# The two halves of each scan group: summed by two TensorE matmuls instead of one GpSimd addition, with step orders and dataless matmuls set anew

## The chip, the cores and the metric

The kernel runs on one core of one Trainium2 chip. The metric is the device time of one execution in microseconds (us), median over the runs. It is set against the same kernel before the change.

## The reference, cut to what matters

The program runs 16 batch elements through four blocks: (a) a selective state-space layer, (b) a routed feed-forward layer, (c) a gated delta rule with an inversion of triangular matrices, and (d) attention with a mixture of eight experts. The change is in block (a). There each of 256 inner channels has 16 states:

```
def step(h, inp):
    dt_t, B_t, C_t, u_t = inp
    dA = jnp.exp(dt_t[:, :, None] * A)
    h = h * dA + (dt_t * u_t)[:, :, None] * B_t[:, None, :]
    y = jnp.einsum('bcs,bs->bc', h, C_t)
    return (h, y)
_, ys = jax.lax.scan(step, h0, xs)
y = jnp.swapaxes(ys, 0, 1) + u * D_skip
```

The sum over the 16 states `s` in the line of `y` is what the change moves from one engine to another.

## The kernel before, in words

**The scan.** Channels lie on the 128 partitions in two blocks (`CB = 2`), time (256) along the free axis. The 16 states are taken in eight groups of two (`SG = 2`, `NG = 8`). A group is a tile of 128 x 1024 float32: two states by two channel blocks by 256 time steps. For group st:

- TensorE spreads the row of B over all partitions (`spread` into bank 0), and the row of C (into bank 1).
- ScalarE makes `decay` (L664, four instructions). VectorE makes `drive` (L1378) from bank 0, runs the recurrence into `state[st % 2]` (L1390), and in `a_read` multiplies that state by C in place (L1398).
- GpSimd adds the two halves of the read-out state into `ypart` (L558), and TensorE adds `ypart` into bank 2 with an identity as weights (L887, one matmul 128x512 float32; the trace has two records for each float32 matmul).

There are two `state` buffers. So the recurrence of group st may only overwrite its buffer once the sum of group st-2 has read it. After the last group `a_y` (L1404) takes bank 2.

**The order of work.** There is no scheduler at run time. Each engine runs its own fixed list of steps: the loop over elements runs the first half (blocks a, b and the projections of c; letter x) of element i among the second half (the rest of c, and d; letter y) of element i-1. A string of x and y for each engine (`TURNS`) says whose next step comes. Within a half the steps keep their order. Every engine works in order and waits at semaphores (`wait_ge`). The first half of element 0 runs alone ahead of the loop, the second half of the last element alone behind it.

Beside the scans in the loop stands the inversion of block c: for each of five levels and two chunks, TensorE's `lev_Z`, VectorE's masking `lev_Z` (L1564), TensorE's `lev_TT` (both L1020 on TensorE) and VectorE's transposition `lev_T` (L1560); then `c_R`, `c_top`, `c_low`, `c_X`, `c_U`, `c_O`, `c_S`, `c_kS`, which apply it.

**Dataless matmuls.** `keep_warm` (L1040) issues matmuls whose result nobody reads, ahead of some of TensorE's steps; the table `WARM` says how many at which step, 50 in an element.

Of the kernel before, what the change touches and what calls it, by code (L numbers as in the profile page):

```python
# [114 lines left out]
for e in range(E1):  # L115
    EXPERTS += [("d_down", e, 0), ("d_down", e, 1)]
    if e + 2 < E1:
# [11 lines left out]
        "yyyyyxyxyyyyyyxxyyyyyxyyyyxyxyyyxyxyyyyxxyyyxxyyxxyyxxyxyxxyxxxxyxyxxyyxxxxyxxxyyxyyyxyyxyyxxyyy"  # L129
        "yyxyxyyyyxyyxyyxyyxyyxyyyxxyyyxxxyyyyyyyxx"),  # L130
    "vector": (
        "xyxyyyxyyxyyxyyyyxxyyyxyyxyyxyyxyyxyyxyyxyyxyyxxyxyxxxyxyxxxxxxyxyxxyxyxxyxyxyxxyxxxyxyyxxxyyyxy"
        "xxxyxxxxyxyxxxyxyxxyyyy"),
    "scalar": (
        "yyxxyyxxxxxyyyxyyyyyxxyyxyyxyxxxyxxyxxxyxxyyyxyxyyxxyxyxyyxyyxxyyxyxyxxxyyxyxyxyyxxx"),
    "gpsimd": (
        "yyxxyyyyyyxxxxxxxxxxyyxyxxx"),
# [4 lines left out]
    ("a_xproj",): 2, ("a_out",): 2, ("b_turn",): 1, ("b_logits",): 1, ("c_prod", 2, 0): 1, ("c_prod", 2, 1): 1,  # L142
    ("lev_Z", 0, 0): 2, ("lev_TT", 0, 0): 2, ("lev_Z", 1, 0): 1, ("lev_TT", 1, 0): 2, ("lev_TT", 1, 1): 1,
    ("lev_Z", 2, 1): 2, ("lev_TT", 2, 0): 1, ("lev_TT", 2, 1): 2, ("lev_Z", 3, 1): 2, ("lev_TT", 3, 0): 2,
    ("lev_TT", 3, 1): 1, ("lev_Z", 4, 1): 1, ("lev_TT", 4, 0): 3, ("lev_TT", 4, 1): 1, ("c_X", 0): 3, ("c_O", 0): 1,
    ("c_S",): 1, ("c_kS",): 1, ("c_top", 1): 1, ("c_low", 1): 1, ("c_O", 1): 2, ("c_turn_o",): 2, ("c_out",): 1,
    ("d_scores",): 2, ("d_turn_p",): 1, ("d_av",): 1, ("d_a",): 2,
# [1599 lines left out]
```

## Time and profile before

| what | value |
|---|---|
| device time, median of 3 runs | 2814.28 us (2812.36 to 2824.87) |
| the profiled execution's own time | 2817.26 us |
| its span | 2815.5 us |
| TensorE matmuls busy | 2434.8 us, 86% of the span |
| VectorE busy | 2208.3 us, 78% |
| ScalarE busy | 1197.7 us, 43% |
| GpSimd busy | 605.6 us, 22% |
| mean granted TensorE clock | 0.931 of full speed |
| DMA, mean | 8 GB/s |

Two engines are busy most of the span, and neither all of it. A busy share is a mean over stages with different limits, so what an edit is worth has to be read from the stage in which it lies. The profiled execution stands 3.0 us above the median.

### The profile page before, as it was taken

How to read it: one execution, taken by the hardware profiler on the slowest of the kernel's cores; microseconds unless marked ns; L12 is line 12 of the kernel's file. 1: busy time of each engine (PE TensorE's matmuls, PEld its weight loads, DVE VectorE, ACT ScalarE, POOL GpSimd, SP SyncE). 2: the span in 40 equal slices, each digit the busy share in tenths (PEclk: the TensorE clock that was granted, in tenths of full speed). 3: DMA queues.
4: the chain of work that ended last, by engine and by line, in shares of the span. 5: the costliest groups of instructions: out<-in, count | busy, mean ns of one | idle time of the engine just before them, and what ended most of it. 6: DMA issues, size and time to landing. Idle time of an engine off the chain costs nothing.

```text
span 2815.5 us, 60867 instructions
## 1 busy us (share of the span) xinstructions
PE 2434.8 (86%) x22584; PEld 1890.6 (67%) x22584; DVE 2208.3 (78%) x5056; ACT 1197.7 (43%) x2697; POOL 605.6 (22%) x465
## 2 busy tenths in 40 slices
PE   4688989888898888989888898988889888898987
PEld 2466767667686766768667686766768666676875
DVE  6677887878879787887978779787887978788742
ACT  3233536435263542536444253543526354353612
POOL 2122221221322122231222222122131212223100
PEclk7689999989999999999999999999999999999987
DMA  4000000000000000000000000000000000000000
GB/s 132 4 2 3 7 4 1 8 3 7 3 7 2 3 8 3 7 4 1 8 3 8 3 7 4 1 8 3 7 3 7 2 3 8 3 7 2 1 6 2
DMA packets 24831, 21.41 MB, mean 8 GB/s; under 512 B 7217, under 2 KB 21570, under 8 KB 24530
## 3 DMA queue, kind: packets, MB, share of 16 engines
q1 hardware_dynamic: 24530, 17.26, 2.2%
q8 instruction: 205, 3.36, 0.5%
q14 instruction: 96, 0.79, 0.1%
HBM read 15.13 MB, written 2.13 MB: 6 GB/s over the span
## 4 chain that ended last, share of the span: by engine, by line
issue 42%; PE 25%; DVE 23%; POOL 6%; ACT 1%; DVEq 0%; POOLq 0%; ACTq 0%
PE banks L1048 4%; PE banks L887 3%; PE banks L1020 3%; DVE wide L1390 3%; PE banks L1012 2%; DVE wide L1398 2%; DVE inv L1560 2%; POOL lg L562 2%; DVE inv L1564 2%; DVE wide L1378 2%; POOL rq L534 2%; PE banks L1001 1%; PE banks L1040 1%; DVE inv L1551 1%; PE banks L864 1%
## 5 line engine op out<-in xcount | busy, mean ns | idle before, releaser
L558 POOL TENSOR_TENSOR wide<-wide 128x512 f32<-128x512 f32 x128 | 215.3, 1682 | 782.0 <-DVE wide L1398 428.4
L1513 DVE SCALAR_TENSOR_TENSOR wide<-pad,conv,wide 128x256 f32<-128x256 f32 x864 | 369.5, 492 | 0.0
L1390 DVE TENSOR_TENSOR_SCAN wide<-wide 128x1024 f32<-128x1024 f32 x128 | 294.3, 2300 | 1.9 <-ACT wide L664 0.3
L1040 PE MATMUL banks<-hideb,identb 128*128 128x512 bf16 x800 | 276.1, 402 | 0.0
L1184 PE MATMUL banks<-inv,up 128*128 128x256 f32 x1024 | 265.9, 391 | 0.0
L1194 PE MATMUL banks<-down,inv 128*128 128x128 f32 x2048 | 257.2, 277 | 0.0
L1194 PEld LDWEIGHTS banks<-down,inv 128*128 128x128 f32 x2048 | 250.7, 192 | 5.9
L1020 PEld LDWEIGHTS banks<-inv 64*64 64x64 f32 x5120 | 164.4, 136 | 111.4 <-issue 111.4
L792 ACT ACTIVATE inv<-banks,up1b 128x256 f32<-128x256 f32 x512 | 206.7, 481 | 65.0 <-PE banks L1184 63.3
L1020 PE MATMUL banks<-inv 64*64 64x64 f32 x5120 | 182.2, 222 | 57.8 <-DVE inv L1564 57.8
L664 ACT ACTIVATE wide<-small,a_neg 128x255 f32<-128x255 f32 x512 | 214.4, 496 | 35.7 <-DVE wide L1390 35.5
L1184 PEld LDWEIGHTS banks<-inv,up 128*128 128x128 f32 x1024 | 184.6, 193 | 21.0 <-issue 0.2
L745 ACT COPY inv<-banks 128x512 f32<-128x512 f32 x160 | 91.3, 580 | 242.0 <-DVE inv L1560 209.5
L1020 PEld LDWEIGHTS banks<-inv,mats 64*64 64x64 f32 x5120 | 163.8, 136 | 35.4 <-issue 35.4
L1020 PE MATMUL banks<-inv,mats 64*64 64x64 f32 x5120 | 180.6, 221 | 4.6 <-DVE inv L1557 4.6
L1378 DVE TENSOR_TENSOR wide<-banks,small 128x1024 f32<-128x1024 f32 x128 | 154.2, 1205 | 3.4 <-PE banks L864 3.4
L534 POOL TENSOR_TENSOR vscale<-vscale,expo 128x16 f32<-128x16 f32 x16 | 46.3, 2895 | 506.8 <-DVE rq L1522 506.8
L1398 DVE TENSOR_TENSOR wide<-banks,wide 128x1024 f32<-128x1024 f32 x128 | 154.2, 1204 | 1.0
L1689 DVE SCALAR_TENSOR_TENSOR inv<-banks,gt,inv 128x128 f32<-128x128 f32 x256 | 77.1, 342 | 98.9 <-PE banks L1194 98.9
L864 PE MATMUL banks<-bc,sel3b 96*128 96x256 bf16 x512 | 100.5, 285 | 55.9 <-DVE wide L1378 31.4
L968 PEld LDWEIGHTS banks<-ones_col,wide 128*128 128x128 f32 x1024 | 135.0, 200 | 9.4 <-issue 2.2
L887 PE MATMUL banks<-wide,con 128*128 128x512 f32 x256 | 138.6, 634 | 0.3 <-POOL wide L558 0.3
(277 smaller groups left out, 4846.7 us busy)
## 6 DMA issues: line engine op xcount, KB each, us to landing
gates_bc<-gate_rows SPq DMA_DIRECT2D x32, 128.0 KB, 2.9
x<-in_x SPq DMA_DIRECT2D x16, 128.0 KB, 2.1
up<-in_W SPq DMA_DIRECT2D x1, 2048.0 KB
out<-xn_y SPq DMA_DIRECT2D x16, 128.0 KB, 2.0
wide<-in_wmod SPq DMA_DIRECT2D x2, 384.0 KB, 5.3
con<-in_con SPq DMA_DIRECT2D x1, 724.0 KB, 4.5
w_k<-in_Wk SPq DMA_DIRECT2D x1, 512.0 KB
w_q<-in_Wq SPq DMA_DIRECT2D x1, 512.0 KB
```

The source lines that it names most:

```text
L558: g.tensor_tensor(ypart[p % 2], r[:, 0:512], r[:, 512:1024], ALU.add).then_inc(a_yp.h, 1)
L664: last = s.activation(decay[st % 2][:, at + 1:at + T], dt[:, c, 1:T], ACT.Exp, scale=a_neg[:, c, st * SG + q:st * SG + q + 1])
L792: s.activation(hm[e % 2][:, m, :], bank(3 + half, T, q * T), ACT.Relu, bias=up1b[:, HB1 * e + m:HB1 * e + m + 1]).then_inc(d_hid.h, 1)
L887: t.matmul(bank(2), ident, ypart[st % 2], start=st == 2, stop=st == NG + 1).then_inc(a_yq.h, 1)
L1020: last = t.matmul(PS[a:b, out, h * HALF:(h + 1) * HALF], weights(h, a, b), values(h, a, b), start=True, stop=True)
L1040: t.matmul(bank(bk), identb[:], hideb[:].unsqueeze(1).broadcast_to([P, HG, P]), start=True, stop=True)
L1184: last = t.matmul(bank(3 + half, T, q * T), up1[:, e, m * P:(m + 1) * P], xxT, start=True, stop=True)
L1194: last = t.matmul(bank(bk, D, j * D), hm[e % 2][:, m, j * P:(j + 1) * P], down1[:, HB1 * e + m, :], start=m == 0, stop=m == HB1 - 1)
L1378: v.tensor_tensor(drive[st % 2].rearrange("p (q c t) -> p q c t", q=SG, c=CB), bank(0).rearrange("p (q t) -> p q t", t=T).unsqueeze(2).bro ...
L1390: v.tensor_tensor_scan(state[st % 2], decay[st % 2], drive[st % 2], 0.0, ALU.mult, ALU.add).then_inc(a_h.h, 1)
L1398: v.tensor_tensor(r, bank(1).rearrange("p (q t) -> p q t", t=T).unsqueeze(2).broadcast_to([P, SG, CB, T]), r, ALU.mult).then_inc(a_rd.h, 1)
L1513: v.scalar_tensor_tensor(dst, src, w, dst, ALU.mult, ALU.add).then_inc(c_conv.h, 1)
```

## The change

In step st of TensorE's `a_read`, one matmul on GpSimd's sum becomes two matmuls, one on each half of the state tile that VectorE has read out, both added into bank 2. GpSimd's step `a_scan` goes, with its buffer `ypart` and its semaphore. VectorE's recurrence of group st now waits for TensorE's semaphore `a_y_summed_ps` of group st-2, where it waited for GpSimd's `a_y_pair`. Three pairs of semaphores are merged into shared ones with counts (`c_solve_ps`, `d_qkv_ps`), with the same waits. The turns of all four engines are written anew, and so is the table of dataless matmuls (51 in an element instead of 50).

```diff
@@ gpsimd
-            def a_scan(i, st):
-                if 1 <= st <= NG:
-
-                    p = st - 1
-                    g.wait_ge(a_rd.h, a_rd.at(i, p + 1))
-                    if p >= 2:
-                        g.wait_ge(a_yq.h, a_yq.at(i, p - 1))
-                    r = state[p % 2]
-                    g.tensor_tensor(ypart[p % 2], r[:, 0:512], r[:, 512:1024], ALU.add).then_inc(a_yp.h, 1)
-
@@ tensor, a_read
                 if st + 1 < NG:
                     t.wait_ge(a_rd.h, a_rd.at(i, st + 1))
                     spread(NS + (st + 1) * SG, 1).then_inc(a_C.h, 1)
-                if st >= 2:
-
-                    t.wait_ge(a_yp.h, a_yp.at(i, st - 1))
-                    t.matmul(bank(2), ident, ypart[st % 2], start=st == 2, stop=st == NG + 1).then_inc(a_yq.h, 1)
+                if 1 <= st <= NG:
+
+                    t.wait_ge(a_rd.h, a_rd.at(i, st))
+                    for n in range(2):
+                        last = t.matmul(bank(2), ident, state[(st - 1) % 2][:, 512 * n:512 * n + 512], start=st == 1 and n == 0,
+                                        stop=st == NG and n == 1)
+                    last.then_inc(a_yq.h, 1)
@@ vector, a_scan
                     if st >= 2:
-                        v.wait_ge(a_yp.h, a_yp.at(i, st - 1))
+                        v.wait_ge(a_yq.h, a_yq.at(i, st - 1))
                     v.tensor_tensor_scan(state[st % 2], decay[st % 2], drive[st % 2], 0.0, ALU.mult, ALU.add).then_inc(a_h.h, 1)
@@ TURNS (gpsimd's shown; tensor, vector and scalar are rewritten too)
     "gpsimd": (
-        "yyxxyyyyyyxxxxxxxxxxyyxyxxx"),
+        "yyxyyyyyyxyyxyxxx"),
```

**What the new orders do on VectorE.** In the loop, around the recurrences of groups 5, 6 and 7 (L1390 before, L1382 after; drive is L1378 and L1370, read-out L1398 and L1390, the solve's small steps the rest), VectorE's list was:

```order
L1390 SCALAR_TENSOR_TENSOR wide<-wide 128x1024 [waits a_y_pair,a_drive,a_decay]
L1375 REGISTER_ALU
L1378 TENSOR_TENSOR wide<-banks,small 128x1024 [waits a_state,a_B_spread]
L1398 TENSOR_TENSOR wide<-banks,wide 128x1024 [waits a_C_spread,a_state]
L1390 SCALAR_TENSOR_TENSOR wide<-wide 128x1024 [waits a_y_pair,a_drive,a_decay]
L1375 REGISTER_ALU
L1378 TENSOR_TENSOR wide<-banks,small 128x1024 [waits a_state,a_B_spread]
L1608 TENSOR_TENSOR inv<-banks,rq 128x256 [waits c_O_ps]
L1398 TENSOR_TENSOR wide<-banks,wide 128x1024 [waits a_C_spread,a_state]
L1582 TENSOR_TENSOR inv<-banks,eGS 128x256 [waits c_kS_ps]
```

and is now:

```order
L1382 SCALAR_TENSOR_TENSOR wide<-wide 128x1024 [waits a_y_summed_ps,a_drive,a_decay]
L1367 REGISTER_ALU
L1370 TENSOR_TENSOR wide<-banks,small 128x1024 [waits a_state,a_B_spread]
L1390 TENSOR_TENSOR wide<-banks,wide 128x1024 [waits a_C_spread,a_state]
L1382 SCALAR_TENSOR_TENSOR wide<-wide 128x1024 [waits a_y_summed_ps,a_drive,a_decay]
L1367 REGISTER_ALU
L1370 TENSOR_TENSOR wide<-banks,small 128x1024 [waits a_state,a_B_spread]
L1390 TENSOR_TENSOR wide<-banks,wide 128x1024 [waits a_C_spread,a_state]
L1600 TENSOR_TENSOR inv<-banks,rq 128x256 [waits c_O_ps]
L1574 TENSOR_TENSOR inv<-banks,eGS 128x256 [waits c_kS_ps]
```

The recurrence's wait names another semaphore, and the small step L1600 (`c_o`, L1608 before) has moved from ahead of the read-out to behind it. Between the read-out of group 5 and the recurrence of group 6 nothing stands, before and after.

Around group 3's recurrence, one masking step of the inversion's last level (L1564 before, L1556 after) stood ahead of it and one behind it. VectorE's list now has, from group 2's recurrence to group 3's:

```order
L1382 SCALAR_TENSOR_TENSOR wide<-wide 128x1024 [waits a_y_summed_ps,a_drive,a_decay]
L1370 TENSOR_TENSOR wide<-banks,small 128x1024 [waits a_state,a_B_spread]
L1390 TENSOR_TENSOR wide<-banks,wide 128x1024 [waits a_C_spread,a_state]
L1555 REGISTER_ALU
L1556 TENSOR_TENSOR inv<-banks,con 128x512 [waits c_Z_ps]
L1555 REGISTER_ALU
L1556 TENSOR_TENSOR inv<-banks,con 128x512 [waits c_Z_ps]
L1382 SCALAR_TENSOR_TENSOR wide<-wide 128x1024 [waits a_y_summed_ps,a_drive,a_decay]
```

Both maskings now lie between a read-out and the next recurrence, and none between a recurrence and its read-out. For all six recurrences that wait, the steps between the read-out ahead and the recurrence are now: group 2: two `lev_T`; 3: two `lev_Z`; 4: `c_R`; 5: `c_U`; 6: none; 7: `c_o` and `c_R`.

**What they do on TensorE.** Behind the last product of `c_S` (L1048 before, L1040 after) stands the step that follows group 5's read-out; `spread` is L864 before and L853 after. Before:

```order
L1048 MATMUL banks<-inv,ktok 128x32
L864 MATMUL banks<-bc,sel3b 128x256 [waits a_read]
L864 MATMUL banks<-bc,sel3b 128x256
L887 MATMUL banks<-wide,con 128x512 [waits a_y_pair]
L877 REGISTER_ALU
L864 MATMUL banks<-bc,sel3b 128x256 [waits a_drive]
```

and now:

```order
L1040 MATMUL banks<-inv,ktok 128x32
L853 MATMUL banks<-bc,sel3b 128x256 [waits a_read]
L853 MATMUL banks<-bc,sel3b 128x256
L877 MATMUL banks<-wide,con 128x512 [waits a_read]
L877 MATMUL banks<-wide,con 128x512
L866 REGISTER_ALU
L853 MATMUL banks<-bc,sel3b 128x256 [waits a_drive]
```

The sum is two matmuls in place of one. In front of it stands, as before, the spread of the next C row, which waits for VectorE's read-out of group 5 itself, while the sum is that of group 4.

## Rows read from the trace of the kernel before

**Rows 1.** The page: span, busy engines, and chain that ended last.

```profile
span 2815.5 us, 60867 instructions
...
PE 2434.8 (86%) x22584; PEld 1890.6 (67%) x22584; DVE 2208.3 (78%) x5056; ACT 1197.7 (43%) x2697; POOL 605.6 (22%) x465
...
issue 42%; PE 25%; DVE 23%; POOL 6%; ACT 1%; DVEq 0%; POOLq 0%; ACTq 0%
```

**Rows 2.** Groups by line: busy us, mean ns of one, idle before.

```profile
L1390 DVE TENSOR_TENSOR_SCAN wide<-wide 128x1024 f32<-128x1024 f32 x128 | 294.3, 2300 | 1.9 <-ACT wide L664 0.3
...
L558 POOL TENSOR_TENSOR wide<-wide 128x512 f32<-128x512 f32 x128 | 215.3, 1682 | 782.0 <-DVE wide L1398 428.4 <-PE banks L887 353.6
...
L887 PE MATMUL banks<-wide,con 128*128 128x512 f32 x256 | 138.6, 634 | 0.3 <-POOL wide L558 0.3
```

**Rows 3.** Stretches of one element: length, then busy us of each engine.

```profile
1056.00:1080.00 24.00, 23.82 (x247) 18.01 (x245) 23.47 (x23) 7.35 (x18) 10.03 (x6) 1.00 0.00 1
...
sum 170.00, PE 149.46 PEld 116.84 DVE 140.31 ACT 77.31 POOL 37.80; mean PE 16.61 PEld 12.98 DVE 15.59 ACT 8.59 POOL 4.20
```

**Rows 4.** Timeline after one read-out: start us, length us, engine, line.

```profile
1063.72 1.23 DVE L1398 TENSOR_TENSOR wide<-banks,wide 128x1024 f32<-128x1024 f32 x1
...
1064.96 0.42 DVE L1600 TENSOR_TENSOR inv<-banks,cU 128x256 f32<-128x256 f32 x1
1065.00 0.11 PEld L864 LDWEIGHTS banks<-bc,sel3b 96*128 96x128 bf16 x2 [0.19 <-DVE wide L1398]
1065.01 0.39 PE L864 MATMUL banks<-bc,sel3b 96*128 96x256 bf16 x2
...
1065.23 1.03 PE L887 MATMUL banks<-wide,con 128*128 128x512 f32 x2
...
1065.77 2.28 DVE L1390 TENSOR_TENSOR_SCAN wide<-wide 128x1024 f32<-128x1024 f32 x1
1066.10 0.38 PE L864 MATMUL banks<-bc,sel3b 96*128 96x256 bf16 x2
```

**Rows 5.** Timeline of VectorE and TensorE among inversion steps.

```profile
1037.75 1.15 PE L1020 MATMUL banks<-inv 64*64 64x64 f32 x32 [0.78 <-DVE inv L1564]
...
1043.87 0.67 DVE L1564 TENSOR_TENSOR inv<-banks,con 128x512 f32<-128x512 f32 x1
1044.47 0.70 DVE L1560 STREAM_TRANSPOSE inv<-banks 128x512 f32<-128x512 f32 x1
...
1045.10 1.18 DVE L1398 TENSOR_TENSOR wide<-banks,wide 128x1024 f32<-128x1024 f32 x1
```

**Rows 6.** Timeline of VectorE ahead of the last scan.

```profile
1073.53 0.41 DVE L1608 TENSOR_TENSOR inv<-banks,rq 128x256 f32<-128x256 f32 x1
1073.86 1.21 DVE L1398 TENSOR_TENSOR wide<-banks,wide 128x1024 f32<-128x1024 f32 x1
1074.99 0.41 DVE L1582 TENSOR_TENSOR inv<-banks,eGS 128x256 f32<-128x256 f32 x1
...
1076.11 2.28 DVE L1390 TENSOR_TENSOR_SCAN wide<-wide 128x1024 f32<-128x1024 f32 x1
```

**Rows 7.** Timeline of the end of an element's scans.

```profile
1080.12 2.05 PE L887 MATMUL banks<-wide,con 128*128 128x512 f32 x4
...
1082.21 0.87 DVE L1404 SCALAR_TENSOR_TENSOR small<-small,d_half,banks 128x256 f32<-128x256 f32 x2 [1.55 <-PE banks L887]
```

**Rows 8.** Timeline of the first element, before the loop.

```profile
53.31 1.92 PE L887 MATMUL banks<-wide,con 128*128 128x512 f32 x2
...
55.68 1.22 DVE L1378 TENSOR_TENSOR wide<-banks,small 128x1024 f32<-128x1024 f32 x1 [0.64 <-PE banks L864]
```

**Rows 9.** Timeline of a GpSimd addition beside a scan.

```profile
1039.42 1.27 POOL L558 TENSOR_TENSOR wide<-wide 128x512 f32<-128x512 f32 x1 [20.60 <-DVE wide L1398]
...
1040.47 2.36 DVE L1390 TENSOR_TENSOR_SCAN wide<-wide 128x1024 f32<-128x1024 f32 x1
```

More of the change, by code:

```diff
@@ L128 @@
     "tensor": (
[L129 to L130 removed]
+        "yyyyyxyxyyyyyyxyyxyyyyyxyyyyyyxxyyyxxyyxxyyxxyyyxxyyxxyxxyxyxxxyxxyxxyyxxxxyxxyxyxyyyxyyyxyxxyyy"
+        "yyxyyxyyyxyyxyyxyyxyyxyyyxyxyyxxyyxyyyyyxx"),
     "vector": (
[L132 to L133 removed]
+        "xyxyyyxyyxyyxyyyyxyyxyyyxyyxyyyxyyxyyxyyxxyyxxyxyxyxxxxyyxxyxxxxxyxxyxyxxyxyxxyxyxxxxyyyxxxyyyxy"
+        "xxxyxxyxxxyxxyxxxxyyyyy"),
     "scalar": (
[L135 removed]
+        "yyxxyyxyxxyxyxyyyxxyyyyyxyxyxxyxxxxyxxxyxxyyyyxxyyxxxyyyyxxyyxyxxyxyxyyxxyxxyyxyxyxx"),
     "gpsimd": (
[L137 removed]
+        "yyxyyyyyyxyyxyxxx"),
 }
 WARM = {
[L142 to L147, printed above, removed]
+    ("a_xproj",): 2, ("a_out",): 1, ("b_turn",): 2, ("b_logits",): 2, ("b_coef",): 1, ("c_turn",): 1,
+    ("c_prod", 2, 1): 1, ("c_prod", 3, 0): 1, ("lev_Z", 0, 0): 1, ("lev_Z", 0, 1): 1, ("lev_Z", 1, 0): 1,
+    ("lev_Z", 1, 1): 1, ("lev_TT", 1, 1): 1, ("lev_Z", 2, 1): 1, ("lev_Z", 3, 0): 2, ("lev_Z", 3, 1): 2,
+    ("lev_TT", 3, 0): 1, ("lev_Z", 4, 0): 1, ("lev_Z", 4, 1): 2, ("lev_TT", 4, 0): 1, ("lev_TT", 4, 1): 1,
+    ("c_top", 0): 2, ("c_low", 0): 3, ("c_X", 0): 3, ("c_O", 0): 2, ("c_S",): 1, ("c_kS",): 3, ("c_O", 1): 1,
+    ("c_turn_o",): 1, ("c_out",): 1, ("d_scores",): 1, ("d_turn_p",): 1, ("d_av",): 2, ("d_a",): 2, ("d_gates",): 1,
 }
@@ L264, in build @@
         state = [wide[:, n] for n in (4, 5)]
-        ypart = [wide[:, 7, 512 * n:512 * n + 512] for n in range(2)]
         sp = sb("sp", [P, 9, 16])
@@ L393, in build @@
         c_kS = sig("c_kS_ps"); c_R0, c_R1 = sigs("c_R", 1, 3)
-        c_tp = sig("c_top_ps", 2); c_tx = sig("c_top", 2); c_lp = sig("c_low_ps", 2); c_low = sig("c_low", 2)
-        c_X = sig("c_X_ps", 2); c_U = sig("c_U", 2); c_Uw = sig("c_Uw")
+        c_slv = sig("c_solve_ps", 6); c_tx = sig("c_top", 2); c_low = sig("c_low", 2)
+        c_U = sig("c_U", 2); c_Uw = sig("c_Uw")
         c_Sp = sig("c_S_ps"); c_S = sig("c_S"); c_O = sig("c_O_ps", 2); c_O2 = sig("c_O2_ps")
@@ L398, in build @@
         c_oTp = sig("c_oT_ps"); c_oT = sig("c_oT"); c_out = sig("c_out_ps")
-        d_qk = sig("d_qk_ps"); d_qks = sig("d_qk", 2); d_vp = sig("d_v_ps"); d_v = sig("d_v")
+        d_qk, d_vp = sigs("d_qkv_ps", 1, 1); d_qks = sig("d_qk", 2); d_v = sig("d_v")
         d_sc = sig("d_scores_ps"); d_mx, d_rs, d_p = sigs("d_prob", 2, 1, 2); d_e = sig("d_exp", 2)
@@ L601, in c_rms_ @@
                 power(rms[:].rearrange("p c h -> p (c h)"), 0).then_inc(c_rrms.h, 1)
-            follow(g, TURNS["gpsimd"], dict(a_norm=a_norm, a_scan=a_scan, b_norm=lambda i: rstd(i, 1), b_root=b_root_, c_norm=lambda i: rstd(i, 2),
+            follow(g, TURNS["gpsimd"], dict(a_norm=a_norm, b_norm=lambda i: rstd(i, 1), b_root=b_root_, c_norm=lambda i: rstd(i, 2),
                            c_gate=c_gate, c_gmask=c_gmask, c_roots=c_roots, c_unit=c_unit,
@@ L1061, in c_top @@
                     last = t.matmul(PS[0:HALF, 3 + ch, h * DV:(h + 1) * DV], TTd[ch][0:HALF, h, :], R[0:HALF, h, :], start=True, stop=True)
-                last.then_inc(c_tp.h, 1)
+                last.then_inc(c_slv.h, 1)
             def c_low_(i, ch):
@@ L1070, in c_low_ @@
                                     start=True, stop=True)
-                last.then_inc(c_lp.h, 1)
+                last.then_inc(c_slv.h, 1)
             def c_X_(i, ch):
@@ L1078, in c_X_ @@
                     last = t.matmul(PS[HALF:P, 3 + ch, h * DV:(h + 1) * DV], TTd[ch][HALF:P, h, :], R[HALF:P, h, :], start=True, stop=True)
-                last.then_inc(c_X.h, 1)
+                last.then_inc(c_slv.h, 1)
             def c_O_(i, ch):
@@ L1596, in c_U_ @@
             def c_U_(i, ch):
-                v.wait_ge(c_X.h, c_X.at(i, ch + 1))
+                v.wait_ge(c_slv.h, c_slv.at(i, 3 * ch + 3))
                 if ch == 1:
```

6 lines of the change are left out of this document (3 added, 3 removed).

## The prediction, made before the changed kernel was run

> **What bounds the kernel now.** I read the page first. TensorE's matmuls are busy 86% of the span and VectorE 78%, GpSimd 22%, and the largest share of the chain that ended last is "issue" [rows 1]. So no engine bounds the whole, and the stage in which the edit lies has to be read by itself. The groups by line say what the scans wait for. The 128 recurrences take 2300 ns each, and VectorE sat idle 1.9 us before all of them together. GpSimd's 128 additions take 1682 ns each behind 782.0 us of idle time, which is time that costs nothing. TensorE's sums are 256 records, two for each matmul [rows 2]. The table by stretches then shows the second half of an element's scans, 24 us, with VectorE busy 23.47 and TensorE 23.82 of them, at the full granted clock. Over the whole element of 170 us VectorE is busy 140.31, so that about 30 us of its idle time lie elsewhere [rows 3]. In the scans VectorE thus runs from one instruction into the next, and whatever stops it there moves everything behind it. GpSimd's addition is hidden: the recurrence of group st needs the sum of group st-2, and that was added while the group between them was being computed.
>
> **What goes.** GpSimd's 128 additions take 215.3 us of an engine on which nothing waits inside the scans. Taking them away is worth nothing by itself, but for two places.
> First, an addition can hold up VectorE at SBUF. One recurrence that began 1.05 us into an addition of 1.27 us took 2.36 us [rows 9]; others took 2.28 [rows 4]. That is 0.08 us, twice in an element: 16 x 0.16 = 3 us at most. The Trainium skill (SBUF — State Buffer, section "SBUF: two separate sides") says that the read path shared by the two engines is an exclusive lock, so that a VectorE instruction with two SBUF inputs would stand until GpSimd's addition ends. By it each of those recurrences would have lost 0.22 us (1040.69 less 1040.47), and the removal would give 7 us instead of 3. The trace shows a smaller effect, and I keep 3.
> Second, at the end of an element's scans the addition is in the chain. `a_y` waits 1.55 us, and in that chain stand GpSimd's 1.27 us and then one matmul [rows 7, 9]. Now two matmuls stand there, one more of 0.87 us. That is 0.4 us less; I count 0.3 us, since TensorE comes to them behind `c_low`.
>
> **What comes: a wait with TensorE in it.** The recurrence of group st now waits until TensorE has summed group st-2. TensorE's list does that sum only in the step that begins by waiting for the read-out of group st-1, behind the two spreads of the next C row. So the sum isn't early, however long its data have been there: it starts when the read-out directly ahead of the recurrence ends. The length of that chain, from rows. A read-out ends at 1064.95; the spread starts at 1065.01, 0.06 later, and the sum 0.22 behind it. Its two records last 1.03, and the next matmul starts 0.87 after their start, so two sums take 1.03 + 0.87 = 1.90 [rows 4]. VectorE starts 0.04 after TensorE's end (1082.17 to 1082.21) [rows 7]. That makes 2.22 us behind the read-out. Without a wait VectorE starts an instruction some 0.07 before the end of the one ahead (1044.54 against 1044.47) [rows 5]. So the hole is 2.3 us for each of groups 2 to 7, less what VectorE has to do between read-out and recurrence in its new list:
> Group 2 has two transpositions, start to start 0.63 each: 1.26. Group 3 has two maskings of 0.60: 1.20 [rows 5]. Group 4 has one small `c_R`, of the shape of the `c_o` that takes 0.33 [rows 6]. Group 5 has `c_U`, 0.81 (1064.96 to 1065.77) [rows 4]. Group 6 has nothing. Group 7 has `c_o`, 0.33, and `c_R`, 1.12 (1074.99 to 1076.11): 1.45 [rows 6].
> That is 6 x 2.3 = 13.8 less 5.05: **8.75 us in each element**. Behind the waiting recurrence on VectorE stand the drive, the read-out and all later inversion steps, so TensorE and ScalarE get nothing to do in that time, and it isn't given back.
>
> Smaller parts, each element. Ahead of group 2, TensorE still has two inversion products of about 1.05 us (one is 1.15 from its start to its end [rows 5]) when the read-out is over: 0.3 late. In the new order the second masking of level 2 stands only one masking behind the transposition that its product needs: 1.15 + 0.1 - 0.6 gives 0.65 of waiting, of which I count 0.5, since the steps ahead of it come a little sooner. The end gives back 0.3. Sum: 8.75 + 0.3 + 0.5 - 0.3 = 9.25 us. The loop runs 15 times: **139 us**.
>
> **The first element**, ahead of the loop, has no inversion steps as cover. There a sum's two records take 1.92 us, the length at half clock, and VectorE waits 0.64 us for the spread in each group [rows 8]. At full clock a hole costs 2.3 - 0.64 = 1.66, and at half clock, with TensorE's parts doubled, 0.07 + 0.06 + 0.44 + 1.92 + 1.7 + 0.04 - 0.64 = 3.6. Six of them are 10 to 22 us. I take **18**, nearer the half clock which the row shows; busier matmuls might raise it.
>
> **The rest.** The added matmuls, 128 of 0.87 us, are 111 us of TensorE time. They lie inside the holes that they make, so they aren't counted twice; without the holes they would be covered by the dataless matmuls' idle places only in part. One dataless matmul more in each element is 0.2 us in front of waits: nothing. The merged semaphores keep their waits: nothing. Outside the scans the orders shift by a place or two (`d_norm` behind `b_up` 0, `d_v` behind `b_up` 5, a mixing step behind the scales). VectorE's 30 us of idle time stand there [rows 3], and such a shift can win or lose some tenths. No row prices it. I bound it at 1.5 us won and 1.0 lost in each element and take 0.5 won, since the shifts mostly put work ahead of a wait: 8 us less.
>
> **Sum:** 139 + 18 - 3 - 8 = +146 us. The profiled execution took 2817.3 us, of which 2815.5 are its span, and stands 3 us above the median of 2814.3. With the same difference the profiled run would take 2963 and the median 2960 us, 5.2% more. What this kernel's measurement can tell from no change is about 0.5%, 14 us.
>
> **The rivals.**
> A. *The holes are partly filled* (2.3 us is too long because the C spread and the sum run while VectorE is in its filler, and the retuned rest wins its bound). The sums alone are 1.90 a group: 6 x 1.90 - 5.05 = 6.35, with nothing late, less 0.6 at the end and the 1.5 of the shifts: 4.3 us, 64 in the loop, and 10 ahead of it: about 2885 us. For it speaks that 30 us of idle time lie outside. Against it: each part of the 2.22 us is a row. Chance 0.09 for 2830 to 2890.
> B. *No slower, or faster.* The one mechanism: the new orders win back idle time of VectorE between the scans and the experts, where it is 30 us in an element [rows 3]. It decides from (139 + 18 - 3) / 15 = 10.3 us an element, that is when a third of that idle time goes; at 12 us it would give about 2790. Against it: that idle time stands in chains of small dependent steps over several engines, and the steps moved there moved by one place. Chance 0.05. The lock at SBUF reaches this only by the 3 us above (7 by the page's rule), so it has no case of its own.
> C. *TensorE becomes the bound in the scans.* It is busy 23.82 of 24 us there [rows 3], and the added 0.87 us a group come on top. If it reaches the C spread 0.6 us late in each of the six groups, that adds 3.6 us an element, 54 in all: about 3014 us. Against it: part of that busy time is dataless matmuls, and each hole lets TensorE catch up. Chance 0.10, half of it above 3015.
> The forecast itself has 0.76.
>
> **How the numbers follow.** 2960 is the sum. The forecast's own bounds run from 2890 (rival A's edge) to 3010; with half of rival C the range is 2890 to 3015, which leaves out A, B and the upper half of C, 0.19. Slower by over 0.5% has the forecast, A and C: 0.95. Within 0.5% has 0.02 and faster 0.03, both out of B.
>
> **What would show it.** In the profile after, the recurrence's line should have idle time before it, ended by TensorE's sum: 15 x (8.75 + 0.3) = 136 us and some 25 in the first element, about 160 us where it was 1.9. The longest should be group 6's, 2.3 us inside the loop. TensorE's sum line should have 512 records. A stretch of an element's scans should hold VectorE's work in some 9 us more. The recurrence's own length should fall by no more than 0.02 us on the mean. I would be wrong if that idle time is there and the span isn't longer (B), if it is below 90 us (A), or if the wait ahead of groups 2 to 7 is over 3 us at the full clock (C).

## The result, and the profile after

The changed kernel takes **2999.19 us** (median of 4 runs, 2997.46 to 3007.86) beside 2813.34 us of the kernel before (4 runs): a ratio of 1.065, interval 1.063 to 1.068. That is 186 us more, where 146 were forecast; it lies inside the range of 2890 to 3015, 16 us from its upper end. The profiled span is 2995.7 us where it was 2815.5, 180.2 us more.

The page of the changed kernel: span, busy engines, chain, then two groups by line (busy us, mean ns of one, idle before and its releaser). They answer to [rows 1, 2].

```profile
span 2995.7 us, 61157 instructions
...
PE 2569.1 (86%) x22856; PEld 1955.1 (65%) x22856; DVE 2218.0 (74%) x5056; ACT 1198.9 (40%) x2697; POOL 390.3 (13%) x337
...
issue 42%; PE 27%; DVE 21%; POOL 6%; ACT 1%; DVEq 0%; POOLq 0%; ACTq 0%
...
L1382 DVE TENSOR_TENSOR_SCAN wide<-wide 128x1024 f32<-128x1024 f32 x128 | 292.7, 2287 | 169.6 <-PE banks L877 167.7
...
L877 PE MATMUL banks<-wide,con 128*128 128x512 f32 x512 | 262.0, 637 | 1.5 <-DVE wide L1390 1.5
```

VectorE does the same work in a longer span: 2218.0 us busy, 10 more than before. Most of these 10 are overlap that it lost. In the kernel before, the loop's recurrences of groups 1 to 7 each start 0.08 us before the end of the instruction ahead; a recurrence that waits for TensorE starts after it. Idle time in front of the recurrences went from 1.9 to 169.6 us, and TensorE's sum ended nearly all of it. The sums are 512 records in place of 256.

Around group 6's recurrence in the sixth element the timeline of the changed kernel reads (start us, length us, engine, line, tile and shape, idle before):

```profile
1150.24 1.21 DVE L1390 TENSOR_TENSOR wide<-banks,wide 128x1024 f32<-128x1024 f32 x1
...
1151.52 0.39 PE L853 MATMUL banks<-bc,sel3b 96*128 96x256 bf16 x2 [0.45 <-DVE wide L1390]
...
1151.74 1.88 PE L877 MATMUL banks<-wide,con 128*128 128x512 f32 x4
...
1153.76 2.29 DVE L1382 TENSOR_TENSOR_SCAN wide<-wide 128x1024 f32<-128x1024 f32 x1 [2.31 <-PE banks L877]
```

The read-out ends at 1151.45, the spread starts 0.07 later, the sum 0.22 behind it. The sum's four records last 1.88, and the recurrence starts 0.14 after them: 2.31 us of idle time, in the place forecast and of about the size. In the whole element the six waits are 1.43, 1.11, 1.97, 1.34, 2.31 and 0.85 us. They sum to 9.01 us of idle time. The forecast had 8.75 + 0.3, but it counted 0.07 for the lost overlap in each hole, which the idle column does not show. With it the measured holes cost some 9.5 us (9.01 and 6 x 0.08).

In 5 of the 15 loop elements the wait ahead of group 4 is 3.62 to 3.67 us in place of 1.97. TensorE's timeline there (the fifth element), in the changed kernel:

```profile
950.14 0.39 PE L853 MATMUL banks<-bc,sel3b 96*128 96x256 bf16 x2 [1.60 <-DVE wide L1390]
950.37 1.88 PE L877 MATMUL banks<-wide,con 128*128 128x512 f32 x4
...
956.99 0.47 PE L853 MATMUL banks<-bc,sel3b 96*128 96x256 bf16 x2 [1.81 <-DVE wide L1390]
957.25 3.54 PE L877 MATMUL banks<-wide,con 128*128 128x512 f32 x4
```

And by stretches of the changed kernel, this element's scans first and then the sixth's (length, busy us of PE, PEld, DVE, ACT, POOL, granted clock, DMA):

```profile
928.70:987.90 59.20, 53.92 (x649) 37.05 (x649) 45.48 (x44) 16.80 (x39) 0.00 (x0) 0.94 0.01 2
1109.10:1166.40 57.30, 50.75 (x648) 35.28 (x648) 45.46 (x43) 16.84 (x39) 0.00 (x0) 1.00 0.01 2
```

TensorE had stood idle for 1.60 and 1.81 us inside two holes, and the same four records then took 3.54 us where they take 1.88. The other ten elements have the same two idle times, to 0.01 us, and their sums kept 1.88. The granted clock of the stretch is 0.94 where it is 1.00 in the sixth element: for a while TensorE ran at 1.2 GHz and not 2.4.

**Where the 180 us of span are.** The last recurrence of the first element starts at 96.18 us where it started at 73.5: 22.7 us. From there to the last recurrence of the loop an element takes 178.14 us where it took 167.19: 15 x 10.95 = 164.2 us. The rest is 6.7 us shorter.

### The profile page after: what moved, and what is told of

The parts are those of the page before. It is cut to its first block, busy times and chain, and to the rows that moved or that the text cites. A ratio compares the mean times of both kernels' runs of the same rounds, so it can differ in the third digit from the quotient of the medians.

```text
span 2995.7 us, 61157 instructions
## 1 busy us (share of the span) xinstructions
PE 2569.1 (86%) x22856; PEld 1955.1 (65%) x22856; DVE 2218.0 (74%) x5056; ACT 1198.9 (40%) x2697; POOL 390.3 (13%) x337
## 4 chain that ended last, share of the span: by engine, by line
issue 42%; PE 27%; DVE 21%; POOL 6%; ACT 1%; DVEq 0%; POOLq 0%; ACTq 0%
PE banks L877 7%; PE banks L1012 4%; DVE wide L1390 3%; PE banks L1004 3%; DVE wide L1370 3%; POOL lg L551 2%; PE banks L1032 2%; DVE inv L1556 2%; POOL rq L533 1%; PE banks L853 1%; DVE wide L1382 1%; PE banks L993 1%; DVE inv L1543 1%; PE banks L1061 1%; PE banks L1053 1%
## 5 line engine op out<-in xcount | busy, mean ns | idle before, releaser
L1382 DVE TENSOR_TENSOR_SCAN wide<-wide 128x1024 f32<-128x1024 f32 x128 | 292.7, 2287 | 169.6 <-PE banks L877 167.7
L1032 PE MATMUL banks<-hideb,identb 128*128 128x512 bf16 x816 | 285.3, 401 | 0.0
L877 PE MATMUL banks<-wide,con 128*128 128x512 f32 x512 | 262.0, 637 | 1.5 <-DVE wide L1390 1.5
L533 POOL TENSOR_TENSOR mv_x<-mv_x,expo 128x2 f32<-128x2 f32 x48 | 33.5, 699 | 1541.2 <-DVE mv_x L1257 1541.2
L1012 PEld LDWEIGHTS banks<-inv,mats 64*64 64x64 f32 x5120 | 171.3, 140 | 83.4 <-issue 83.4
L1012 PE MATMUL banks<-inv,mats 64*64 64x64 f32 x5120 | 190.8, 226 | 36.1 <-DVE inv L1549 22.3
L853 PE MATMUL banks<-bc,sel3b 96*128 96x256 bf16 x512 | 97.7, 284 | 124.7 <-DVE wide L1390 93.4
L853 PEld LDWEIGHTS banks<-bc,sel3b 96*128 96x128 bf16 x512 | 39.5, 100 | 196.6 <-DVE wide L1390 103.4
L1390 DVE TENSOR_TENSOR wide<-banks,wide 128x1024 f32<-128x1024 f32 x128 | 155.7, 1216 | 1.0
L1370 DVE TENSOR_TENSOR wide<-banks,small 128x1024 f32<-128x1024 f32 x128 | 153.2, 1197 | 0.0
L1004 PE MATMUL banks<-kq 128*128 128x256 f32 x512 | 145.8, 424 | 0.2 <-DVE mats L1535 0.2
```

The lines of the kernel that those rows point to most:

```text
L877: last = t.matmul(bank(2), ident, state[(st - 1) % 2][:, 512 * n:512 * n + 512], start=st == 1 and n == 0, stop=st == NG and n == 1)
L1004: last = t.matmul(bank(3 + n % 2, 256, y * 256), kq[:, h, 0, ch * P:(ch + 1) * P], kq[:, h, :, ch * P:(ch + 1) * P], start=True, stop=True)
L1012: last = t.matmul(PS[a:b, out, h * HALF:(h + 1) * HALF], weights(h, a, b), values(h, a, b), start=True, stop=True)
L1032: t.matmul(bank(bk), identb[:], hideb[:].unsqueeze(1).broadcast_to([P, HG, P]), start=True, stop=True)
L1370: v.tensor_tensor(drive[st % 2].rearrange("p (q c t) -> p q c t", q=SG, c=CB), bank(0).rearrange("p (q t) -> p q t", t=T).unsqueeze(2).bro ...
L1382: v.tensor_tensor_scan(state[st % 2], decay[st % 2], drive[st % 2], 0.0, ALU.mult, ALU.add).then_inc(a_h.h, 1)
```

## The experiments

Each kernel is set against the kernel before on the same chip. The kernel before has medians of 2813 to 2819 us on them, so a difference between two experiments is uncertain by up to 6 us where they ran on different chips. In the shares below, "idle before the recurrence" is that of all 128.

### Are the holes the loss? Three ways to shorten them

**e1.** In TensorE's `a_read` the sum stands ahead of the next C row's spread.

```diff
             def a_read(i, st):
-                if st + 1 < NG:
-                    t.wait_ge(a_rd.h, a_rd.at(i, st + 1))
-                    spread(NS + (st + 1) * SG, 1).then_inc(a_C.h, 1)
                 if 1 <= st <= NG:
...
                     last.then_inc(a_yq.h, 1)
+                if st + 1 < NG:
+                    t.wait_ge(a_rd.h, a_rd.at(i, st + 1))
+                    spread(NS + (st + 1) * SG, 1).then_inc(a_C.h, 1)
```

> The changed kernel, but in TensorE's step behind a read-out the sum of the group before stands ahead of the C spread and its wait, so that it no longer starts at the read-out. Theory (the recurrence waits for a sum that TensorE's order ties to the read-out just ahead of it): the holes before the recurrences go (167.7 us idle becomes under 40), and some of it comes back as VectorE waiting at its read-outs for C, since TensorE now has some 6.5 us of work between read-outs of groups 4 to 6 where VectorE has 5: about 2880 us, 2850 to 2910. Rival 1 (the added matmul time itself, TensorE as the bound): no better than 2970. Rival 2 (the new orders and their dataless matmuls cost the time): no better than 2960.

Measured: **2900.62 us**, ratio 1.030 (1.027 to 1.033), inside the band of the theory. Changed kernel e1, recurrence's group by line:

```profile
L1382 DVE TENSOR_TENSOR_SCAN wide<-wide 128x1024 f32<-128x1024 f32 x128 | 292.5, 2285 | 70.8 <-PE banks L874 40.8
```

The order of two calls in one step is worth 99 us: the sum now runs as soon as its own data are there. The idle time fell from 169.6 to 70.8, also 99. Of the 70.8, TensorE ends 40.8 and ScalarE's decays end 28.3.

**e2.** A third state buffer, so that group st waits for the sum of st-3.

```diff
-        state = [wide[:, n] for n in (4, 5)]
+        state = [wide[:, n] for n in (4, 5, 7)]
-                    if st >= 2:
-                        v.wait_ge(a_yq.h, a_yq.at(i, st - 1))
+                    if st >= 3:
+                        v.wait_ge(a_yq.h, a_yq.at(i, st - 2))
```

> The changed kernel with a third state buffer (in the block of SBUF that the removed GpSimd sums had), so that the recurrence of group st waits for the sum of group st-3. TensorE's order and its work are untouched. Theory: the holes go just as with the sum put first, 2850 to 2910 us, with no idle time before the recurrences. Rival 1 (TensorE's added time is the bound): 2970 or more, since its work is the same. Rival 2 (orders): 2960 or more.

Measured: **2916.02 us**, ratio 1.036 (1.033 to 1.039), 6 us over its band. TensorE no longer holds up a recurrence, but another engine does. Group by line, and around group 6 the timeline, in e2:

```profile
L1382 DVE TENSOR_TENSOR_SCAN wide<-wide 128x1024 f32<-128x1024 f32 x128 | 291.5, 2277 | 68.0 <-ACT wide L653 66.5
```

```profile
1115.54 0.37 ACT L742 COPY inv<-banks 128x256 f32<-128x256 f32 x1 [7.99 <-PE banks L1040]
1115.81 3.29 ACT L653 ACTIVATE wide<-small,a_neg 128x255 f32<-128x255 f32 x8
1117.54 2.29 DVE L1382 TENSOR_TENSOR_SCAN wide<-wide 128x1024 f32<-128x1024 f32 x1 [3.04 <-ACT wide L653]
```

In the new order ScalarE makes group 6's decays behind a copy of `c_S` that waits 7.99 us for TensorE. In the changed kernel the same pair stands at 1151.10 and 1151.37 and is covered by the hole.

**e5.** The changed kernel with one of the two matmuls: only the first half of each state is summed, and the second is left out of the result.

```diff
-                    for n in range(2):
-                        last = t.matmul(bank(2), ident, state[(st - 1) % 2][:, 512 * n:512 * n + 512], ...)
+                    last = t.matmul(bank(2), ident, state[(st - 1) % 2][:, 0:512], ...)
```

> The changed kernel with only one of the two sum matmuls in each group: the second half of each state tile is left out of the output. Theory: the hole before each recurrence is as long as TensorE's sum, so it shrinks by 0.87 us in each of six groups, 5.2 us an element, with 0.9 us more at the end of an element; but the decays that ScalarE makes late in the new order (seen in the run with three buffers) take over in two of the six groups, so not below some 2905: 2925 us, 2905 to 2945. Were the hole a fixed handoff cost it would stay above 2980.

Measured: **2893.73 us**, ratio 1.026 (1.023 to 1.029), 11 us under its band and 105 us less than the changed kernel. 128 matmuls of 0.87 us are 111 us. So nearly all of TensorE's time for the left-out matmuls had been VectorE's time too, as the forecast's chain says. The idle time before the recurrence fell to 77.8 us, 51.3 of it TensorE's and 25.0 ScalarE's.

### The engine and the orders apart

**e4.** The changed kernel with the turns of TensorE, VectorE and ScalarE and the dataless matmuls of the kernel before (ScalarE's line shown).

```diff
     "scalar": (
-        "yyxxyyxyxxyxyxyyyxxyyyyyxyxyxxyxxxxyxxxyxxyyyyxxyyxxxyyyyxxyyxyxxyxyxyyxxyxxyyxyxyxx"),
+        "yyxxyyxxxxxyyyxyyyyyxxyyxyyxyxxxyxxyxxxyxxyyyxyxyyxxyxyxyyxyyxxyyxyxyxxxyyxyxyxyyxxx"),
...
```

> The changed kernel under the orders and dataless matmuls of the kernel before. Theory: holes as before less other fillers. Between read-out and recurrence stand 1.23, 1.23, 0, 0.81, 0 and 1.12 us, 4.4 in all instead of 5.05, and the sums of groups 1 to 3 come later behind inversion steps: 13.8 - 4.4 = 9.4 us an element and up to 1 more, 2985 to 3015 us. Rival 2 (the orders cost the time): 2830 to 2880 us.

Measured: **3089.03 us**, ratio 1.097 (1.093 to 1.100). Missed, 74 us over the band. The recurrence's group of e4:

```profile
L1382 DVE TENSOR_TENSOR_SCAN wide<-wide 128x1024 f32<-128x1024 f32 x128 | 293.2, 2290 | 262.2 <-PE banks L877 253.3
```

The engine change under the old orders costs 274 us, and the new orders take 90 us off it. TensorE's clock is part of that. e4's list of instructions is that of e7 below, but TensorE is busy 2623.5 us here and 2536.5 there, and in the loop the wait ahead of group 4 is 2.88 us in some elements and up to 6.04 in others.

**e3.** The other half: the kernel before, GpSimd's addition kept, with the new turns of TensorE, VectorE and ScalarE and the new dataless table; GpSimd's turns stay. Its diff is that of e4 with + and - exchanged.

> The kernel before, with GpSimd's additions and one matmul a group, under the new orders of TensorE, VectorE and ScalarE and the new table of dataless matmuls. Theory: no holes before the recurrences, so near the kernel before; the maskings that now wait and the lower clock at the start of block c cost 1 to 2.5 us an element: 2828 to 2855 us. Rival 2 (the orders cost the time): 2950 or more. Rival 1: as the theory.

Measured: **2950.8 us** (2936.21 to 2967.52), ratio 1.050 (1.044 to 1.055). The theory missed it by a hundred; rival 2 (the orders cost the time, 2950 or more) was right. VectorE's waits in e3 (us in total, times, longest):

```profile
DVE wide L1390 <- ACT wide L664: 63.7, 31, 3.9
DVE small L1404 <- PE banks L887: 48.4, 16, 5.4
```

Before, the first was 0.3 us [rows 2] and the second, `a_y` at the end of the scans, 26.3. Together they rose by 85 us. The first is ScalarE's decays behind its copies, as in e2. Other waits of VectorE rose too: the maskings' from 6.9 to 32.5 us, against 14 won at the transpositions, and those for the products of k and q from 20.9 to 37.2. The recurrences themselves take 7 us more, since more GpSimd additions run into them. Two rows of e3 show one:

```profile
1118.49 1.27 POOL L558 TENSOR_TENSOR wide<-wide 128x512 f32<-128x512 f32 x1 [2.63 <-PE banks L887]
...
1119.20 2.70 DVE L1390 TENSOR_TENSOR_SCAN wide<-wide 128x1024 f32<-128x1024 f32 x1 [2.17 <-ACT wide L664]
```

The new orders are thus worse by 136 us where there are no holes, and better by 90 where there are.

### With the holes gone, what is next?

**e7.** Three buffers (e2), with the turns and dataless matmuls of before (e4).

> TensorE's sums and three state buffers under the orders and dataless matmuls of the kernel before. Theory (the engine change costs time only through the recurrence's wait; what is left with three buffers under the new orders is theirs): 2805 to 2845 us, no idle time before the recurrences. Rival 1 (the added 111 us of matmul time count by themselves): 2900 or more.

Measured: **2909.50 us**, ratio 1.032 (1.029 to 1.035). The theory missed; rival 1, TensorE's added time, was right. The group by line, two of VectorE's waits, and the timeline around group 1, of e7:

```profile
L1382 DVE TENSOR_TENSOR_SCAN wide<-wide 128x1024 f32<-128x1024 f32 x128 | 292.2, 2283 | 1.9 <-ACT wide L653 0.3
```

```profile
DVE wide L1370 <- PE banks L853: 60.0, 65, 2.3
DVE inv L1585 <- PE banks L1061: 50.5, 17, 4.7
```

```profile
1080.58 1.88 PE L877 MATMUL banks<-wide,con 128*128 128x512 f32 x4
...
1082.83 1.15 PE L1012 MATMUL banks<-inv,mats 64*64 64x64 f32 x32
1083.91 0.39 PE L853 MATMUL banks<-bc,sel3b 96*128 96x256 bf16 x2
...
1084.34 1.22 DVE L1370 TENSOR_TENSOR wide<-banks,small 128x1024 f32<-128x1024 f32 x1 [0.99 <-PE banks L853]
```

No recurrence waits any more, and the span is still 92 us over the kernel before. The drive and block c's small steps wait for TensorE instead. The B row's spread stands behind the sum in TensorE's list; the sum doubled, so the spread is late. Under these orders the third buffer takes 180 us off (3089 to 2909).

**e9.** The sum first (e1) under the orders of before (e4).

> TensorE's sums with the sum ahead of the C spread, two state buffers, under the orders of the kernel before. Theory: the sum no longer waits for the read-out just ahead, but TensorE must reach it before VectorE ends that read-out; it has 6 us of work between read-outs of groups 5 and 6 where VectorE has 4.4 to 5.9, so holes of about 1 us stay in two or three groups: 2835 to 2880 us. Rival 1: 2900 or more.

Measured: **3031.31 us**, ratio 1.076 (1.073 to 1.079). The theory missed it by 150 us; rival 1 had only 2900 or more. The timeline of e9 ahead of group 4's recurrence in the sixth element, one of its longest waits:

```profile
1125.32 1.15 PE L1012 MATMUL banks<-inv 64*64 64x64 f32 x32 [1.79 <-DVE inv L1556]
...
1126.28 1.75 PE L1053 MATMUL banks<-inv 64*64 64x32 f32 x16
...
1127.96 3.78 PE L874 MATMUL banks<-wide,con 128*128 128x512 f32 x4
...
1131.87 2.29 DVE L1382 TENSOR_TENSOR_SCAN wide<-wide 128x1024 f32<-128x1024 f32 x1 [5.23 <-PE banks L874]
```

Under these orders the sum stands behind inversion products that wait for VectorE themselves, and here it ran at half clock too (3.78). Moving it within its step gains 58 us on e4 (3089 to 3031), and no more, since the step itself is late; the same edit was worth 99 us under the new orders.

**e10.** e2 with ScalarE's turns of before, the line that e4's diff shows.

> The changed kernel with three state buffers, all as in that run but ScalarE's turns, which are those of the kernel before (the decays of groups 4 and 6 ahead of the copies of the inversion's last level and of c_S). Theory (with the holes gone, what holds VectorE in the new orders is ScalarE's decays behind those copies, 66.5 us of idle time): 2850 us, 2835 to 2880. Rival (the rest of the orders, TensorE's and the dataless matmuls, costs it): 2905 to 2920, as with ScalarE's new turns.

Measured: **3018.51 us**, ratio 1.070 (1.067 to 1.073). Missed, by the theory and by the rival. The decays are on time (recurrences idle 1.9 us), but now ScalarE's copies for the inversion stand behind them. One such chain in e10: decays, copy, TensorE's product, transposition.

```profile
1108.35 3.29 ACT L653 ACTIVATE wide<-small,a_neg 128x255 f32<-128x255 f32 x8
...
1111.84 1.05 ACT L734 COPY inv<-banks 128x512 f32<-128x512 f32 x2
1112.52 1.97 PE L1012 MATMUL banks<-inv 64*64 64x64 f32 x32 [4.76 <-issue]
...
1114.52 0.72 DVE L1552 STREAM_TRANSPOSE inv<-banks 128x512 f32<-128x512 f32 x1 [5.35 <-PE banks L1012]
```

TensorE sat idle 4.76 us, and its product then took 1.97 us where it takes 1.15 at full clock. One engine's old list among three new ones is 102 us worse than four new ones.

**e11.** e2 with only two of ScalarE's steps moved: the decays of group 4 ahead of one inversion copy, those of group 6 ahead of the copy of `c_S`.

```diff
-        "yyxxyyxyxxyxyxyyyxxyyyyyxyxyxxyxxxxyxxxyxxyyyyxxyyxxxyyyyxxyyxyxxyxyxyyxxyxxyyxyxyxx"),
+        "yyxxyyxyxxyxyxyyyxxyyyyxyyxxyxyxxxxyxxxyxxyyyyxxyyxxxyyyyxxyyxyxxyxyxyyxxyxxyyxyxyxx"),
```

> Three state buffers under the new orders, with two places of ScalarE's list exchanged: the decays of group 4 ahead of the inversion's last copy, those of group 6 ahead of the copy of c_S. Theory: the 66.5 us that the recurrences waited for ScalarE with three buffers go, and TensorE's list is then what VectorE meets next: 2850 to 2885 us. Rival (ScalarE's wait only covered one of TensorE of the same length): 2905 to 2920.

Measured: **2923.82 us**, ratio 1.036 (1.033 to 1.038). The theory missed, and the rival was right to within 4 us: ScalarE's 66.5 us ahead of the recurrences went, and the time stayed. VectorE's waits in e11 show where:

```profile
DVE inv L1585 <- PE banks L1061: 80.4, 32, 5.1
...
DVE wide L1370 <- PE banks L853: 25.6, 20, 2.3
```

**e12.** e7, with the sums of groups 0 to 5 moved from `a_read` into TensorE's `a_scan`, behind the spread of the next B row.

```diff
+            def add_state(i, p):
+                t.wait_ge(a_rd.h, a_rd.at(i, p + 1))
...
             def a_scan(i, st):
...
                     spread((st + 1) * SG, 0).then_inc(a_B.h, 1)
+                if 2 <= st <= NG - 1:
+                    add_state(i, st - 2)
             def a_read(i, st):
...
-                if 1 <= st <= NG:
...
+                if st in (NG - 1, NG):
+                    add_state(i, st - 1)
```

> Three state buffers, orders and dataless matmuls of the kernel before, and each of the sums of groups 0 to 5 behind the next B spread instead of ahead of it. Theory: with three buffers the sum no longer holds the recurrence but the drive, whose B spread stands behind it (3.5 us idle at four drives in an element), so that goes: some 50 us less than 2909, if TensorE isn't simply full: 2850 to 2870. Rival (TensorE is full there, wherever the sum stands): 2900 to 2915.

Measured: **2895.14 us**, ratio 1.027 (1.025 to 1.029), 25 us over the theory's band and 5 under the rival's. The drive's 60 us of waiting went (no idle time ended by a spread is left on its line) and the time fell by 14. The wait moved on to the small steps of `c_low`. In e12:

```profile
DVE inv L1589 <- PE banks L1065: 83.5, 32, 4.7
```

**e13.** e12 without 24 of the 50 dataless matmuls in an element, those that stand beside the scans.

```diff
-    ("lev_Z", 1, 0): 1, ("lev_TT", 1, 0): 2, ("lev_TT", 1, 1): 1,
-    ("lev_Z", 2, 1): 2, ("lev_TT", 2, 0): 1, ("lev_TT", 2, 1): 2, ("lev_Z", 3, 1): 2, ("lev_TT", 3, 0): 2,
-    ("lev_TT", 3, 1): 1, ("lev_Z", 4, 1): 1, ("lev_TT", 4, 0): 3, ("lev_TT", 4, 1): 1, ("c_X", 0): 3, ("c_O", 0): 1,
-    ("c_S",): 1, ("c_kS",): 1, ("c_top", 1): 1, ("c_low", 1): 1, ("c_O", 1): 2,
+    ("lev_Z", 1, 0): 1, ("lev_TT", 1, 0): 2, ("c_O", 1): 2,
```

> As the run with the sums behind the B spread, and without the 24 dataless matmuls an element that stand beside the scans from the inversion's second level on (0.215 us each, 5.2 us an element). If TensorE's time is what is left, this gives it back: 2800 to 2840 us. If the dataless matmuls only fill idle time and hold the clock up, it is the same or slower: 2860 to 2900.

Measured: **2854.86 us**, ratio 1.012 (1.011 to 1.014). 24 fewer in each of 16 elements give 40 us, which lies between what the two theories had. Page, waits, and the end of the scans, in e13:

```profile
PE 2452.5 (86%) x22456; PEld 1915.3 (67%) x22456; DVE 2206.9 (77%) x5056; ACT 1199.1 (42%) x2697; POOL 390.8 (14%) x337
```

```profile
DVE inv L1584 <- PE banks L1060: 59.7, 32, 3.5
```

```profile
1090.77 3.70 PE L855 MATMUL banks<-wide,con 128*128 128x512 f32 x8
...
1094.40 1.11 PE L1060 MATMUL banks<-inv,mats 64*64 64x32 f32 x16
...
1095.55 0.42 DVE L1584 TENSOR_TENSOR inv<-inv,banks 64x256 f32<-64x256 f32 x1 [2.80 <-PE banks L1060]
```

TensorE's busy time fell from 2533.9 to 2452.5 us and VectorE's wait for `c_low` from 83.5 to 59.7. Here time taken off TensorE comes back, half of it. What is left at the end of the scans is two groups' sums in a row (3.70 us) ahead of `c_low`. This is the fastest version here with the whole sum on TensorE, and it is still 1.2% slower than the kernel before.

### Half clock inside the holes

**e6.** The changed kernel with four dataless matmuls each ahead of the waits of `a_read` 2 and 3, into an unused bank.

```diff
+    ("a_read", 2): 4, ("a_read", 3): 4,
             def a_read(i, st):
+                keep_warm(7, "a_read", st)
```

> The changed kernel with four dataless matmuls (0.86 us) ahead of the waits of TensorE's read-out steps 2 and 3, where it sits idle 1.6 and 1.8 us inside the holes. Clock theory: in some elements the granted clock falls to half during the sum behind those holes (3.54 us instead of 1.88), and work in the idle time keeps it up: the waits of 3.7 us before group 4's recurrence go in the elements that have them, some 10 us in all: 2985 to 2993 us, and no recurrence waits over 2.5 us inside the loop. Rival (the half clock there has another cause, such as what ran before the scans): no change, 2994 to 3005.

Measured: **2976.70 us**, ratio 1.056 (1.054 to 1.058). That is 22 us less than the changed kernel's 2999 (28 if each is set against the kernel before on its own chip), more than expected. TensorE's timeline of e6 at the place shown above:

```profile
953.01 0.39 PE L854 MATMUL banks<-bc,sel3b 96*128 96x256 bf16 x2 [0.84 <-DVE wide L1392]
953.24 1.88 PE L879 MATMUL banks<-wide,con 128*128 128x512 f32 x4
```

The idle time is 0.84 us in place of 1.81, and the sum is at full clock in every loop element. The recurrences' idle time ended by TensorE fell from 167.7 to 158.6, 9 us, which fits 5 x 1.7. Another part is in block c: its products of k and q (L1004, L1006 in e6) ran 424 ns each in the changed kernel, 389 before, and 393 here. In the changed kernel, and then in e6, by line:

```profile
L1004 PE MATMUL banks<-kq 128*128 128x256 f32 x512 | 145.8, 424 | 0.2 <-DVE mats L1535 0.2
```

```profile
L1006 PE MATMUL banks<-kq 128*128 128x256 f32 x512 | 132.8, 393 | 1.3 <-DVE mats L1537 1.3
```

VectorE's wait for them fell from 35.4 to 28.0 us. So the changed kernel also came to block c at a lower clock. That gives 16 of the 22 us; 3.9 more lie behind the loop's last recurrence, and nothing explains them.

## Why the prediction was right, and where not

**Right: the mechanism and its length.** The recurrence waits for a sum that starts when the read-out ahead ends. The forecast's net waits for groups 2 to 7 were 1.34, 1.10, 1.97, 1.49, 2.30 and 0.85; the idle times measured are 1.43, 1.11, 1.97, 1.34, 2.31 and 0.85. From its first recurrence to its last the sixth element takes 51.5 us where it took 42.5: the 9 more that were forecast. That this chain costs the time is shown by undoing it: 99 us with the sum first (e1), 83 with a third buffer (e2), 105 with half the sum (e5). The idle time ahead of the recurrences was forecast at about 160 us, and is 169.6. Rivals A (holes partly filled) and B (won back elsewhere) fell with it.

The terms of the sum, in us of the whole program. The measured ones are read from the traces, but for the line of the shifts outside the scans, which is what is left of the difference.

| term | forecast | measured |
|---|---|---|
| waits of groups 2 to 7, 15 elements (late start included) | 136 | 9.01 x 15 = 135 idle |
| overlap lost at each of these waits | in the 136, at 0.07 | 6 x 0.08 x 15 = 7 |
| second masking of level 2 | 7.5 | 11 |
| end of the scans | -4.5 | -4 |
| TensorE at half clock in group 4's hole | none | 5 x 1.7 = 8.5 |
| first element | 18 | 22.7 |
| lock at SBUF | -3 | -1.7 |
| shifts outside the scans | -8 | 0.55 x 15 = +8 |
| behind the last recurrence of the loop | none | -6.7 |
| sum | 146 | 180 of span |

**Mis-sized.** The sum was 34 us short of the span's 180 (40 of the median's 186), and nearly every term missed to the same side. "I bound it at 1.5 us won and 1.0 lost in each element and take 0.5 won" had the wrong sign. Outside the scans an element lost about 0.55 us, inside the bound of 1.0 lost; one visible part is the slower products of k and q (389 to 424 ns; 411 in e3, under the same lists but without the holes). The masking term has two waits, 0.74 and 0.76 us in the sixth element, against which one of the transpositions' waits went: the masking's waits rose from 6.9 to 32.4 us, the transpositions' fell from 17.8 to 3.8, which leaves 11.5. In the first element the 3.6 us of a hole at half clock were right: they are 4.2 less the 0.64 us that VectorE waited for the spread before, and the holes measured are 3.82 to 4.22 us, 24.3 in all, with no wait for the spread left (3.4 us before). What was low is the choice of 18, between full and half clock: all six holes were at half clock. For the lock, the recurrence's mean fell from 2300 to 2287 ns, 1.7 us in all; the rows' 3 was the nearer estimate.

**Misread: the lock at SBUF.** The forecast found that the trace shows a smaller effect than a lock would. It shows a lock. In the kernel before, 28 recurrences began with 0.20 to 0.22 us of a GpSimd addition left, and in e3 54 began with 0.17 to 0.56 us left. Every one of the 82 ended 2.14 to 2.16 us after that addition's end, whatever was left (in the rows of e3 above 1121.90 less 1119.76); an undisturbed one takes 2.28. So a recurrence stands still until the addition is over, but for its first 0.13 us or so. The Trainium skill (SBUF — State Buffer, section "SBUF: two separate sides") says that whichever of the two instructions starts first keeps the shared port pair for its whole length and the other fully blocks. These traces agree with it. The forecast's 7 us by that rule left out the 0.13: 0.21 less 0.13 is the 0.08 that it read from the rows.

**Left out: the clock.** The forecast took the loop at full clock throughout, since the stretch of before shows 1.00 [rows 3]. But a hole of VectorE is also idle time of TensorE, and that brought it down to half clock in a third of the elements. e6 shows it: with work in the idle time the long waits ahead of group 4 go, 9 us, and the run is 22 us shorter.

**What holds for this pair alone.** Of the added matmuls the forecast says "They lie inside the holes that they make, so they aren't counted twice", and it priced the new orders at almost nothing. Both were right for this pair of engine and orders only. The parts don't add up to it:

| | orders of before | new orders |
|---|---|---|
| sum on GpSimd | 2814 | 2951 (e3) |
| sum on TensorE | 3089 (e4) | 2999 |
| sum on TensorE, three buffers | 2909.5 (e7) | 2916 (e2) |

274 for the engine and 136 for the orders would make 410; together they are 186. One reading is that the new orders are fitted to the holes: they put fillers into them (group 7's `c_o` and `c_R`, group 3's second masking), and ScalarE's decays behind copies that a hole covers. Without holes these decays are late; e2 and e3 show that. For the fillers no run stands alone. The clock is a second part that no run separates: the runs that came out slowest against their theories (e3, e4, e9 and e10) also have the lowest mean granted clocks, 0.909 to 0.920 in their profiles, where the changed kernel has 0.932 and e7 0.939. The forecast came near because it worked out the pair as it stands, on its own list, and not the parts.

**Rival C was wrong here and right one step on.** TensorE isn't the limit while the holes last: no loop wait of the recurrences at full clock is over 2.31 us. When they are gone (e7, e11, e12) VectorE waits for other work of TensorE instead, and 76 to 105 us stay, about the 111 us of the added matmuls. e13 takes 81 us off TensorE's busy time, and 40 us come off the kernel's. Adding half of rival C widened the range from 3010 to 3015, which the result of 2999 didn't need.

**Open.** e3's runs spread over 31 us, and I didn't find why. That the last 35 us or so of e13 over the kernel before are sums ahead of `c_low` and block c's waits is read from its trace, not tested. The kernel before wasn't run without the 24 dataless matmuls that e13 leaves out, so how much of the 40 us it would have won too isn't known. Why the clock fell in 5 of 15 elements and not in the ten with the same idle times is open as well. Whether GpSimd's work in some other form would fit e13 wasn't tried.

## What to carry to other kernels

When work moves from an idle engine to a busy one, ask first what new thing its consumer waits for, and in which step of the new engine's list that stands: here the sum stood behind a wait for the read-out directly ahead, and the order of two calls in one step was worth 99 us under one set of lists and 58 under another. Where each engine has a fixed list, price an edit and its new lists together. An order tuned to one set of waits is a loss under another, and one old list among new ones can be worse than all new (102 us, e10). A stall of one engine is idle time of the next, so look whether its clock falls there, and expect that the next limit is close behind: removing the 167.7 us of waits gave back 83.
